# MoE outputs added to DRAM tables by indirect accumulating DMAs, and a shorter router chain, in a four-layer kernel

## The reference

```python
scores = sigmoid(x @ router_w.T);  sc = scores + e_bias
# 3 best of 8 groups of 4 experts, then the 4 best of 32 experts
topk_w = scores[topk] / (sum + 1e-20) * 2.5
# expert e takes its first C = 160 tokens, in order of token
Y = (silu(Xp @ W_gate) * (Xp @ W_up)) @ W_down        # per expert, [160, 256]
out[slots_token] += Y * slots_w[:, None]
shared = (silu(x @ shared_gate.T) * (x @ shared_up.T)) @ shared_down.T
x = layernorm(x + out + shared)
```

## Time and profile before

| | |
|---|---|
| Median of 3 runs | 2558.71 us (2549.15 to 2562.81) |
| Profiled execution, its span | 2652.0 us |
| Mean granted TensorE clock in it | 0.881 of full |
| Busy share | PE 77%, PEld 67%, DVE 63%, ACT 41%, POOL 31% |
| SP's DMA queue | 80,912 packets, 97.06 MB |

### The profile page before, as it was taken

The page is one execution under the profiler, slowest core; times in us unless marked ns, Lnnn a source line. Parts: engine busy times, 40 slices in busy tenths (PEclk is TensorE's granted clock), DMA queues, the critical chain, the costliest instruction groups (busy, mean ns, idle before and its releaser), DMA issues. The chain is left out here.

```text
span 2652.0 us, 39910 instructions
## 1 busy us (share of the span) xinstructions
PE 2029.2 (77%) x12272; PEld 1774.7 (67%) x12272; DVE 1674.2 (63%) x4576; ACT 1081.1 (41%) x2760; POOL 824.7 (31%) x778
## 2 busy tenths in 40 slices
PE   7999999999987996799888889899974555457000
PEld 5877877877866884688888778788874444356000
DVE  8867767667754553477777777777763445445443
ACT  5433333333323331376666666666662111146000
POOL 1222322322320000133333333333320433431776
PEclk9999999999998997799999999999997665679555
DMA  3100000000002123000000000000003111146101
GB/s 120 32 25 24 0 24 24 15 9 24 16 9 94 48 64 106 30 6 17 22 13 13 12 13 16 13 21 12 9 9 128 65 37 35 34 133 204 36 25 30
DMA packets 93344, 103.68 MB, mean 39 GB/s; under 512 B 16670, under 2 KB 84710, under 8 KB 92592
## 3 DMA queue, kind: packets, MB, share of 16 engines
q1 hardware_dynamic: 80912, 97.06, 11.5%
q0 software_dynamic: 12288, 5.08, 0.8%
HBM read 86.55 MB, written 44.04 MB: 49 GB/s over the span
## 5 line engine op out<-in xcount | busy, mean ns | idle before, releaser
L224 POOL TENSOR_TENSOR rwkv_gate<-rwkv_key,rwkv_gate 128x512 f32<-128x512 f32 x128 | 206.3, 1612 | 569.1 <-DVE rwkv_key L406 569.1
L1094 POOL TENSOR_TENSOR mla_probs<-mla_probs,mla_row_inv 128x512 f32<-128x512 f32 x192 | 199.7, 1040 | 471.0 <-DVE mla_row_inv L1391 470.8
L1376 DVE CUSTOM_DVE_ANT_0 mla_masked<-mla_score,mla_mask 128x256 f32<-128x256 f32 (+1 forms) x512 | 157.3, 354 | 164.6 <-PE mla_score L1586 115.0
L291 ACT ACTIVATE rwkv_gate<-rwkv_r 128x512 f32<-128x512 f32 x128 | 76.4, 597 | 417.9 <-DVE rwkv_o_low L343 417.9
L1205 ACT ACTIVATE mla_probs<-mla_masked,mla_least 128x256 f32<-128x256 f32 (+1 forms) x512 | 227.4, 447 | 35.1 <-DVE mla_least L1376 31.1
L392 DVE TENSOR_TENSOR rwkv_kv<-rwkv_v,rwkv_key 128x512 f32<-128x512 f32 x128 | 88.0, 688 | 178.6 <-PE rwkv_v L441 110.5
L2023 POOL DMA_INDIRECT slots<-moe_x_rows,moe_slot_now x128 | 124.8, 975 | 198.1 <-DVE moe_slot_at L2270 110.0
L458 PE MATMUL rwkv_out<-rwkv_w_high,rwkv_o_high 128*128 128x256 f32 x512 | 146.3, 286 | 38.1 <-DVE rwkv_o_low L343 38.1
L1221 ACT ACTIVATE mla_p_high<-mla_pt 128x512 fp32r<-128x512 f32 x192 | 114.3, 595 | 136.7 <-PE mla_pt L1595 132.0
L398 DVE TENSOR_TENSOR_SCAN rwkv_state<-rwkv_decay_w,rwkv_kv 128x256 f32<-128x256 f32 x256 | 163.4, 681 | 4.1
L1586 PE MATMUL mla_score<-mla_k_high,mla_q_high 128*128 128x256 f32 (+1 forms) x512 | 157.6, 308 | 1.8 <-DVE mla_cq_low L1309 1.8
(11 more groups left out here) (360 smaller groups left out, 6597.5 us busy)
## 6 DMA issues: line engine op xcount, KB each, us to landing
moe_w_raw<-in_experts SPq DMA_DIRECT2D x32, 384.0 KB, 4.4
rwkv_w_raw<-in_rkvo SPq DMA_DIRECT2D x16, 512.0 KB, 3.4
slots<-moe_zeros SPq DMA_DIRECT2D x40, 128.0 KB, 1.8
moe_e_rows<-slots SPq DMA_DIRECT2D x32, 160.0 KB, 3.9
slots_out<-moe_y_rows SPq DMA_DIRECT2D x32, 160.0 KB, 3.8
mla_w_raw<-in_mla_heads SPq DMA_DIRECT2D x4, 1152.0 KB, 7.7
rwkv_x_in<-in_x_t SPq DMA_DIRECT2D x16, 256.0 KB, 4.0
rwkv_x_res<-in_x SPq DMA_DIRECT2D x8, 512.0 KB, 3.9
```

Source lines behind the costliest of these rows:

```text
L224: nc.gpsimd.tensor_tensor(gate[:, c % 2, :], key[:, c % 2, :], gate[:, c % 2, :], ALU.mult).then_inc(gated_done, 1)
L1094: nc.gpsimd.tensor_tensor(unit, unit, row_inv[:, v % 3, 0:len(heads)].rearrange("p (h a) -> p h a", a=1) .to_broadcast([P, len(heads), key ...
L1376: last = nc.vector.tensor_tensor_reduce(out=masked[:, v % 2, i * keys:(i + 1) * keys], in0=score_ps[v % 2][:, i * keys:(i + 1) * keys], in ...
```

## The change

The output rows no longer go back to the tokens by a gather at the end. A row in `slots` now is 289 words: 256 features, 32 router weights and the token's number; each expert loads its rows with the number, and its own weight column as a second DMA of single words (`e_weight`). ACT multiplies by the weight as it copies. POOL adds the two 80-row halves of each expert into four DRAM tables `sums` of 4224 rows, one for each parity of the expert and half, with indirect accumulating DMAs; each waits for the last one into the same table. Rows of `slots` that no token fills carry weight zero and a number from 4096 up, past the tokens. SP clears the four tables with `slots`, before block 1's rows. `load_slots` moves by one expert and waits until the additions of the expert that had the buffer are done, since they read the token numbers there. The combine stage loads four tables' rows for each pair and adds them with four DVE instructions. DVE's chain has 23 links, `member` comes ahead of `add_shared` and `shared_hidden`, and a few instructions are merged.

```diff
@@ SP
-                    for a in range(SLOTROWS // P):
-                        sp.dma_start(slots_dram[a * P:(a + 1) * P, :], zeros[:, :]).then_inc(slots_zeroed, 16)
+                    half = SLOTROWS // CH2 // 2
+                    for a in range(2):
+                        sp.dma_start(slots_dram[a * half * CH2:(a + 1) * half * CH2, :]
...
+                                     .to_broadcast([CH2, half, ROW])).then_inc(slots_zeroed, 16)
+                    for a in range(SUMS):
+                        sp.dma_start(sums_dram[a].rearrange("(b p) d -> p b d", p=P),
...
+                                     .to_broadcast([P, SUMROWS // P, D])).then_inc(sums_zeroed, 16)
...
             def load_slots(e, i, r):
                 if not (isinstance(e, int) and e < RING):
-                    sp.wait_ge(e_turned, e - RING + 1)
+                    wait_first(sp, e_turned, e - RING + 1, passed)
+                    for a in range(2):
+                        wait_first(sp, y_added[r][a], 16 * i, passed)
                 sp.dma_start(e_rows[:, r, :, :], slot_rows(slots_dram, e)).then_inc(slots_in[r], 16)
+                sp.dma_start(e_weight[:, r, :, :], slot_rows(slots_dram, e)[:, :, bass.ds(e + D, 1)],
...
             def experts(e, i, r):
                 if is_expert(e + RING):
                     load_w(e + RING, i + 1, r)
-                    load_slots(e + RING, i + 1, r)
-                if late(e):
-                    store_y(*ring_of(i, r, -1))
+                if is_expert(e - 1 + RING) and late(e):
+                    before, i1, r1 = ring_of(i, r, -1)
+                    load_slots(before + RING, i1 + 1, r1)
...
+                for a in range(SUMS):
+                    sp.dma_start(y_in[:, r, a, :, :], sums_dram[a][bass.ds(n * 2 * P, 2 * P), :]
...
@@ POOL
+            def add_rows(e, i, r):
+                pool.wait_ge(y_copied, e + 1)
+                for a in range(2):
+                    if not (isinstance(e, int) and e < SUMS // 2):
+                        _, before, r2 = ring_of(i, r, -(SUMS // 2))
+                        wait_first(pool, y_added[r2][a], 16 * before + 16, passed)
+                    nc.gpsimd.indirect_dma_start(
+                        sums_dram[r * 2 % SUMS + a],
+                        bass.IndirectOffsetOnAxis(e_rows[:, r, a, IDCOL:ROW].bitcast(U32), 0),
+                        y_rows[:, r, a, :], None, bounds_check=SUMROWS - 1, oob_is_err=True,
+                        compute_op=ALU.add).then_inc(y_added[r][a], 16)
@@ ACT
-                nc.scalar.activation(y_rows[:, r, :, :], route_ps[0:CH2, :].rearrange("p (a d) -> p a d", a=2),
-                                     ACT.Copy).then_inc(y_copied, 1)
+                for a in range(2):
+                    last = nc.scalar.activation(y_rows[:, r, a, :], route_ps[0:CH2, a * D:(a + 1) * D], ACT.Copy,
+                                                scale=e_weight[:, r, a, :])
+                last.then_inc(y_copied, 1)
@@ DVE
+                    pair = total[:, bass.ds(2 * n, 2), :]
+                    nc.vector.tensor_tensor(pair, y_in[:, r, a, :, :], pair, ALU.add).then_inc(chain, 1)
```

More of the change, by code:

```diff
@@ L1760, with moe_phase @@
 PAST_END = 65536.0
-ROUTER_LINKS = 29
-def moe_phase(nc, ident_dram, router_w, e_bias, counts_dram, earlier_dram, w_experts, w_shared, zero_rows,
-              x3, slots_dram, y_dram, out):
+ROUTER_LINKS = 23
+ROW = D + E + 1
+IDCOL = D + E
+SUMS = 4
+SUMROWS = TOKENS + P
+def moe_phase(nc, ident_dram, router_w, e_bias, counts_dram, earlier_dram, tokens_dram, w_experts, w_shared,
+              empty_rows, x3, slots_dram, sums_dram, out):
     with ExitStack() as ctx:
@@ L1825, in moe_phase @@
         w_part = both("w", [P, 2, EW])
-        e_rows = s.sb("e_rows", [CH2, RING, 2, D])
+        e_rows = s.sb("e_rows", [CH2, RING, 2, ROW])
+        e_weight = s.sb("e_weight", [CH2, RING, 2, 1])
         e_part = both("e", [P, 2, KD, CAP])
@@ L1887, in moe_phase @@
         y_copied = s.sem("y_copied")
[L1888 to L1891, removed]
+        y_added = [[s.sem(f"y_added{r}_{a}") for a in range(2)] for r in range(RING)]
+        sums_in = [s.sem(f"sums_in{r}") for r in range(RING)]
         added = s.sem("added")
+        sums_zeroed = s.sem("sums_zeroed")
         stats_done = s.sem("stats_done")
@@ L2029, in _ @@
             blocks(pool, scatter)
[L2032 to L2051, removed]
+            pool.wait_ge(sums_zeroed, 16 * SUMS)
+            def add_rows(e, i, r):
[9 more added lines that the diff above has]
+                        compute_op=ALU.add).then_inc(y_added[r][a], 16)
+            rings(pool, E, add_rows)
             def rsqrt(n, par):
@@ L2343, in combine @@
             def combine(n, i, r):
-                dve.wait_ge(gathered[r], 16 * 2 * TOPK * (i + 1))
-                for k in range(TOPK):
-                    for t in range(2):
-                        if k > 0:
-                            dve.wait_ge(chain, NB * ROUTER_LINKS + 8 * n + 2 * (k - 1) + t + 1)
-                        row = total[:, bass.ds(2 * n + t, 1), :].rearrange("p a d -> p (a d)")
-                        last = nc.vector.scalar_tensor_tensor(
-                            row, y_in[:, r, t, k, :], weight[:, bass.ds((2 * n + t) * TOPK + k, 1)], row,
-                            ALU.mult, ALU.add)
-                        last.then_inc(chain, 1)
-                wait_first(dve, chain, NB * ROUTER_LINKS + 8 * n + 8, passed)
+                dve.wait_ge(sums_in[r], 16 * SUMS * (i + 1))
+                for a in range(SUMS):
+                    if a > 0:
+                        dve.wait_ge(chain, NB * ROUTER_LINKS + SUMS * n + a)
+                    pair = total[:, bass.ds(2 * n, 2), :]
+                    nc.vector.tensor_tensor(pair, y_in[:, r, a, :, :], pair, ALU.add).then_inc(chain, 1)
+                wait_first(dve, chain, NB * ROUTER_LINKS + SUMS * n + SUMS, passed)
                 for t in range(2):
@@ L2516, in rwkv_attention_moe_program @@
     x3 = nc.dram_tensor("x3", (TOKENS, D), F32).ap()
-    slots = nc.dram_tensor("slots", (SLOTROWS, D), F32).ap()
-    slots_out = nc.dram_tensor("slots_out", (SLOTROWS, D), F32).ap()
+    slots = nc.dram_tensor("slots", (SLOTROWS, ROW), F32).ap()
+    sums = [nc.dram_tensor(f"sums{a}", (SUMROWS, D), F32).ap() for a in range(SUMS)]
     rwkv_phase(nc, a["x_t"], a["x"], a["rkvo"], a["decay"], a["first"], a["mixes"], x1)
@@ L2522, in rwkv_attention_moe_program @@
                     a["rope_q"], a["rope_k"], a["mask"], x2, x3)
-    moe_phase(nc, a["ident"], a["router_w"], a["e_bias"], a["counts"], a["earlier"], a["experts"], a["shared"],
-              a["zeros"], x3, slots, slots_out, out)
+    moe_phase(nc, a["ident"], a["router_w"], a["e_bias"], a["counts"], a["earlier"], a["tokens"], a["experts"],
+              a["shared"], a["empty"], x3, slots, sums, out)
 def constants():
```

145 lines of the change are left out of this document (72 added, 73 removed).

## The result

| | before | after |
|---|---|---|
| Median | 2560.76 us (4 runs) | 2617.32 us (2609.05 to 2620.53, 4 runs) |
| Ratio after to before | | 1.0227, 95% interval 1.0200 to 1.0254 |
| Profiled execution: span | 2652.0 us | 2613.2 us (the execution took 2614.99) |
| Mean granted clock | 0.881 | 0.874 |

The change costs 56.6 us; 53 were forecast. The profiled execution of after lies at its median, that of before 91 us above its own. What those 91 us are matters for one term and is settled by the experiments.

What follows compares the result with a forecast made beforehand. It saw POOL's gathers pacing the combine stage, experts near PE's pace and no engine near full in the blocks. Terms 51 - 15 + 122 - 105 = +53 gave 2612 us for the median, range 2548 to 2690.

Steps and rivals of the forecast that it cites:

- the stalls: Token blocks: ACT's second gate stands 13.39 us, in seven blocks; believed mostly the profiled execution's own.
- clearing: SP's queue: 23.2 MB cleared ahead of block 1's rows delays PE's second turn to 2108; +51 us.
- chain: DVE's router chain in the token blocks gets shorter; -15 us, bounds 5 and 30.
- experts: Expert stage: reloading a slot buffer waits for POOL's additions, making a loop; +122 us, ends +74 and +203.
- combine: Combine stage: 16 pairs at 5.65 us, in all 107 us of the former 211; -105 us.
- its two cases: Blocks: with the stall 4 us a block saved, 30 in all; without it the saving ends at POOL's pace.
- The step of 14.25 us: Expert loop: two experts cost L + W, 10.05 us from addition to reloaded turn plus 4.2 of PE work.
- the landing: Expert loop: time for an accumulating scatter to land, taken as 3.0 us, with 2.1 and 6 as ends.
- A slot: Expert stage: PE's work of turn(e+1), hidden(e) and out(e-1), taken as 4.2 us, near the lower clock.
- The faster one: Rival, expert loop: short reload, step 9 us, experts +45, total 2535; decides under a 9.6 us step; chance 0.13.
- The much slower one: Rival, expert loop: additions land in 6 us and the reload meets weights; step 20, total 2693; chance 0.17.
- Block 1's rows did not pass the clearing: No-change rival, SP's queue: block 1's rows pass the clearing or it is covered, 51 us unpaid, 2561; chance 0.10.

Runs made afterwards that it cites:

- before_again: The kernel before, unchanged, run once more for its profile: one execution of 2571.56 us with a span of 2569.5, on the chip of 2555 us.
- old_chain_2: The changed kernel with the old router chain, beside the change on a chip with the stalls: 2723.02 us against 2697.39.
- change_again: The changed kernel, unaltered, run again on a chip with the stalls: 2697.39 us against 2646.34 for the kernel before, ratio 1.0185.

## Why the prediction was right

Its 2612 us stood against 2617.32. The four terms are measured between the profiles of after and `before_again`, neither of which has the stalls. Their marks are the phase's first load, PE's second turn, the first load of rows and the last copy, `before_again` first (after's second turn stands above):

```profile
2030.10 0.38 SPq L1945 DMA_DIRECT2D moe_xt_rows<-x  x1
2068.01 1.97 PE L2394 MATMUL moe_gate<-moe_ident,moe_xt_rows 128*128 128x128 f32 x8 [7.85 <-DMA moe_xt_rows<-x]
2261.52 1.80 SPq L1980 DMA_DIRECT2D moe_e_rows<-slots  x4
2358.61 0.59 ACT L2129 ACTIVATE moe_y_rows<-moe_route 80x512 f32<-80x512 f32 x1 [1.08 <-PE moe_route L2491]
```

```profile
2017.59 0.38 SPq L1945 DMA_DIRECT2D moe_xt_rows<-x  x1
2284.07 0.33 SPq L1991 DMA_DIRECT2D moe_e_rows<-slots  x1
2510.57 0.83 ACT L2152 ACTIVATE moe_y_rows<-moe_route,moe_e_weight 80x256 f32<-80x256 f32 x2 [1.08 <-PE moe_route L2494]
```

| term | forecast | measured | by |
|---|---|---|---|
| clearing | +51 | +49.8 | phase's first load to PE's second turn: 87.75 - 37.9 |
| chain | -15 | -14.8 | second turn to first load of rows: 178.7 - 193.5 |
| experts | +122 | +129.4 | first load of rows to last copy: 226.5 - 97.1 |
| combine | -105 | -108.3 | last copy to the end: 102.6 - 210.9 |
| sum | +53 | +56.1 | medians: +56.6 |

**Clearing.** 74.8 us from the first clearing DMA to the turn; the forecast had 73 at 318 GB/s with 3.9 for the load. The rate was a mean of two: while `slots` was cleared the windows show 253 GB/s, while the tables were, 374. That 318 came near their mean is luck: it was the average of a queue with other work. The 248 of the earlier trace rows was no measure of the engines either: SP spent 21.12 us on 40 issues of 128 KB, 0.53 each, with the engines at 0.71.

```profile
2031.00:2053.00 22.00, 14.94 (x56) 12.48 (x54) 10.71 (x46) 6.31 (x9) 0.00 (x0) 0.66 0.93 253
2054.00:2098.00 44.00, 0.00 (x0) 0.00 (x0) 0.00 (x0) 0.00 (x0) 0.00 (x0) 0.50 1.06 374
```

The Trainium skill, "DMA: Bandwidth & Descriptors", Specifications, has about 358 GB/s as a core's limit. The second window lies 4% above it, the first far below. By the page the term was +43, by the rows +51, and 49.8 came.

**The chain.** The term was right, and its two cases too: bounded by POOL without the stalls, more where they hold (30 forecast; 25.6 in `old_chain_2`, and 262.4 us for the blocks of `change_again`, 2107.27 to 2369.62, against 285.9). That the 15, a choice between 5 and 30, came within 0.2 us is chance. Wrong was the belief that the stalls are mostly the profiled execution's own: `before_again` was profiled without them, and two chips show them timed and profiled. The forecast came through because only the blocks' term touched them. Had the medians been taken on such a chip, the blocks' term would be -23.5; there the change cost 51.1 us.

**The experts.** The step of 14.25 us was 14.7. Inside it two sizes were off and nearly cancelled, which is luck: the two issues take 3.3 us instead of 2.25 (the addition's 0.49 each), the landing 2.1 instead of 3.0. A slot was 4.6 us instead of 4.2: PE stayed at the half clock (0.52 over the stage), at which the earlier trace rows have 4.37 from turn to turn. Fourteen steps of 0.47 more make 6.6 of the 7 us missing.

**The combine stage.** A pair took 4.95 us instead of 5.65. I had charged each addition 0.2 us for the wait on the one before; four of 0.69 take 2.87 in all, so most of that wait lies under the addition itself. Around the pairs it was longer: 15.4 us to the first addition instead of 12.4, and 13.0 for the last pair instead of 9.9.

**The rivals.** The faster one needed a step under 9.6 us; the floor of 11.0 from plain transfers held, since even plain writes gave 13.2. The much slower one (landing in 6 us) did not come: additions landed in 2.1 us, and with the DMA engines at 0.47 the loads of `e_rows` took 2.4 us in the median, where before they took 3.9. Block 1's rows did not pass the clearing.

## What to carry over

When a buffer has to be kept for an operation at the end of a chain of four engines, the buffer's reload joins that chain into a loop: give the small thing that it reads (here four bytes a row) a ring of its own, and leave the large load free. Put bulk work on a queue where what stands behind it is not needed soon, and look at each later load again after splitting it: pieces in a bad place gave back 34 of 46 us. Compare kernels only within one chip, or each with the kernel before on its own, and a profile with a median only if both could be from the same chip.

## What was not expected of the hardware

- Three chips ran the same kernel in 2555, 2650 and 2646 us, each within 0.5% of its median. The difference is one kind of stall of ACT and DVE, which delays the start of each of seven bursts of 16 indirect DMAs by up to 13.7 us in the change (`change_again`) and is released by something that the profile calls remote. Each chip was seen once.
- SP is held up at the issue of large DMAs: 50.43 us for four of 4.3 MB, 11.10 us for one of 512 KB behind them.
- An accumulating indirect DMA of 80 rows costs POOL 1.49 us to issue, a plain one 0.995, and lands 2.1 us after its issue instead of 1.6.
- Rows of 1156 bytes were cleared at 253 GB/s, rows of 1024 bytes at 374, in neighbouring stretches of one queue. What makes the difference was not tried, and the length of the rows is not shown to be it: the first DMAs also come from 80 partitions instead of 128.
